# A pacing wait in front of the scatters of a token-routed projection is taken out (one core)

## The reference

```
x = x + 0.5 * ffn(layernorm(x))     # phase 1 of the routed projection, then attention
x = x + encoder_block(layernorm(x)) # 16 heads of 16, relative positions, 2 linear layers
x = x + 0.5 * ffn(layernorm(x))     # phase 2 of the routed projection, then attention

def ffn(x):                         # q, k, v each by a routed two-layer projection
    for f in (q, k, v):
        leaf = walk of a binary tree of depth 4 by the signs of x . node_w[cur] + node_b[cur]
        out_f = relu(x @ w1[leaf] + b1[leaf]) @ w2[leaf] + b2[leaf]   # 256 -> 64 -> 256
    return softmax(q @ k.T / 16) @ v
```

## Time and profile before

| | |
|---|---|
| median of 3 runs | 3535.45 us (3533.83 to 3539.51) |
| the profiled execution | 3535.45 us, span 3533.8 us |
| PE busy | 3043.8 us, 86% of the span |
| DVE busy | 2089.9 us, 59% |
| ACT busy | 1758.2 us, 50% |
| POOL busy | 863.8 us, 24% |
| SP's transfers, share of 16 DMA engines over the span | 33.8% |
| Pool's transfers, same | 7.4% |

### The profile page before, as it was taken

How to read it: one execution, slowest core, us unless ns; L and a number is a source line. 1 busy time by engine, 2 the same in 40 slices (tenths; PEclk the granted TensorE clock), 3 DMA queues, 4 the chain that set the end, 5 groups by cost and what they waited for, 6 DMA issues and landing times. The chain is left out here.

```text
span 3533.8 us, 56088 instructions
## 1 busy us (share of the span) xinstructions
PE 3043.8 (86%) x21058; PEld 1867.1 (53%) x21058; DVE 2089.9 (59%) x3115; ACT 1758.2 (50%) x3413; POOL 863.8 (24%) x1448
## 2 busy tenths in 40 slices
PE   7377579999688999999999999999677377679999
PEld 6256368888343333333333333333346266468888
DVE  3222245544347999999999999995243222245554
ACT  1133233333121888888888888888341133333333
POOL 5531232100013222222222222211025531232100
PEclk9999789999795999999999999999885699789999
DMA  7488421100557444444444455440321488421100
GB/s 259 142 279 249 147 59 52 43 27 20 191 204 88 54 58 56 56 57 56 56 56 56 61 60 61 54 52 9 107 96 50 149 276 255 137 59 53 44 26 22
DMA packets 498902, 338.91 MB, mean 96 GB/s; under 512 B 174333, under 2 KB 473372, under 8 KB 498638
## 3 DMA queue, kind: packets, MB, share of 16 engines
q1 hardware_dynamic: 464718, 251.45, 33.8%
q0 software_dynamic: 33920, 83.93, 7.4%
HBM read 207.93 MB, written 130.97 MB: 96 GB/s over the span
## 5 line engine op out<-in xcount | busy, mean ns | idle before, releaser
L1355 DVE TENSOR_REDUCE mx_ha<-s_ps_ha 128x2 f32<-128x1024 f32 x1024 | 1242.4, 1221 | 106.1 <-PE s_ps_ha L1262 101.8
L1420 ACT ACTIVATE probs_ha<-s_ps_ha 128x512 f32<-128x512 f32 x2048 | 1108.8, 595 | 218.7 <-PE s_ps_ha L1273 84.6
L1262 PE MATMUL s_ps_ha<-ks_ha,qs_ha 48*128 48x512 f32 x2048 | 760.9, 455 | 18.7 <-DMA ks_ha<-parts_d 13.2
L1273 PE MATMUL s_ps_ha<-qs_ha,ks_ha 50*128 50x512 f32 x2048 | 750.7, 446 | 0.9 <-ACT probs_ha L1420 0.2
L1284 PE MATMUL o_ps_ha<-probs_ha,vs_ha 128*32 128x256 f32 (+1 forms) x7936 | 650.1, 400 | 21.4 <-DVE oT_ha L1382 21.4
L1262 PEld LDWEIGHTS s_ps_ha<-ks_ha,qs_ha 48*128 48x128 f32 x2048 | 314.9, 191 | 453.5 <-DVE mx_ha L1355 360.1
L640 PE MATMUL s_ps_a<-kT_a,qT_a 128*128 128x512 f32 x1536 | 398.3, 407 | 2.9 <-issue 2.9
L673 PE MATMUL o_ps_a<-v_a,probsT_a 128*128 128x512 f32 x1024 | 380.4, 411 | 7.2 <-DVE probsT_a L702 6.9
L399 DVE COPY y_p<-y_ps_p 128x256 f32<-128x256 f32 x282 | 117.5, 424 | 447.6 <-PE y_ps_p L496 285.0
L614 POOL DMA_INDIRECT rows_a<-ys_d,slots x192 | 181.7, 946 | 792.7 <-PE turn_ps_a L628 511.6
L1284 PEld LDWEIGHTS o_ps_ha<-probs_ha,vs_ha 128*32 128x32 f32 x7936 | 156.8, 108 | 381.0 <-issue 176.1
(11 more groups left out here) (178 smaller groups left out, 3439.5 us busy)
## 6 DMA issues: line engine op xcount, KB each, us to landing
xs_p<-xs_d SPq DMA_DIRECT2D x66, 512.0 KB
ys_d<-y_p SPq DMA_DIRECT2D x66, 512.0 KB
qs_ha<-parts_d SPq DMA_DIRECT2D x192, 128.0 KB, 6.1
ks_ha<-parts_d SPq DMA_DIRECT2D x192, 128.0 KB, 6.9
wa_p<-in_wa SPq DMA_DIRECT2D x282, 65.5 KB
wb_p<-in_wb SPq DMA_DIRECT2D x282, 65.0 KB
parts_d<-parts_hp POOLq DMA_DIRECT2D x32, 512.0 KB, 3.1
xs_d<-y_p SPq DMA_DIRECT2D x15, 1024.0 KB, 11.1
```

The lines of the kernel that those rows point to most:

```text
L1262: nc.tensor.matmul(s1_ps[:, e % BANKS, :], qs[0:QKROWS, n % SLOTS, c, :], ks[0:QKROWS, n % SLOTS, g * 4:(g + 1) * 4, :].rearrange("p c t - ...
L1273: nc.tensor.matmul(out, ks[LOW:LOW + KR, n % SLOTS, c, :], qs[LOW:LOW + KR, n % SLOTS, g * 4:(g + 1) * 4, :].rearrange("p c t -> p (c t)") ...
L1355: nc.vector.reduce_max(mx[:, at:at + 2], s1_ps[:, e % BANKS:e % BANKS + 2, :], AX_X).then_inc(s1_free, 1)
L1420: nc.scalar.activation(probs[:, (n + c) % (LATE + 1), g * 512:(g + 1) * 512], s2_ps[:, turn % TURNS, :], ACT.Exp).then_inc(s2_free, 1)
```

## The change

The wait of Pool for `turned` in front of the scatters of passes 2 and 3 is removed, in both phases. The waits for the blanking of `xs_d` (first phase only) and for the slots of the pass stay, and so does everything on the other engines.

```diff
@@ -278,8 +278,6 @@
                     pool.wait_ge(filled[f], 16 * -(-SEG // (YB * GROUP)))
                 pool.wait_ge(slot_step, 3 * (k + 1))
                 for t in range(GT):
-                    if k >= 1:
-                        pool.wait_ge(turned, (k - 1) * SEG + t + 1)
                     pool.indirect_dma_start(xs_d[f], bass.IndirectOffsetOnAxis(slots[:, f, t:t + 1], 0),
                                             xn[:, t, :], None).then_inc(scattered[f], 16)
```

## The result

The changed kernel takes 3678.11 us (median of 4 runs, 3675.05 to 3680.67), the kernel before on the same chip 3534.64 (4 runs, 3532.32 to 3539.51). The ratio is 1.0404, 95% interval [1.0385, 1.0422]: 143.5 us slower, where 4.6 was forecast. The profiled execution took 3675.87 us, its span 3674.2.

What follows compares the result with a forecast made beforehand. Projection tiles were taken as paced by DMA landings, with engine demand rising to 1.04 beside dense scatters. Per phase +1.9 us net collision and +0.4 at the start, twice, gave +4.6 on 3535.45: 3540 us, range 3530 to 3553.

Steps and rivals of the forecast that it cites:

- the removed wait is worth 0 by itself: Pool's scatters in the projection: over 20 us of slack each, so starting them earlier gives back no time.
- the term for the collision: Projection tiles beside dense scatters: 8.0 us paid less 6.1 freed, net +1.9 us per phase.
- Pool's 96 scatters in one run ending near 224 us: Pool in each phase: scatters issued unbroken, waits for PE gone, one every 1.265 us.
- The first turn later by less than 1 us: Projection start: three scatters now run before the first `xs` load, costing 0 to 1.0 us, taken as 0.4.
- What is given back: Projection tiles after 224 us run free of scatters: 60.5 tiles by 0.10 us, 6.1 us per phase.
- The term u: Share of time the DMA engines reach beside dense scatters, taken as 0.955: 1.90 us a tile, 8.0 us paid per phase.
- the engine time per tile: DMA engine time one projection tile needs: taken as 21.0 engine-us, between 20.4 and 21.4 from the rows.
- The rule of the Trainium skill: DMA engines go round robin over queues; early scatters would fill gaps, full use, net -2.6 us per phase.
- rival (b): Projection scatters cost the same whenever they come: 3536 us; full engine use without start cost, 3530 us; chance 0.18.
- (c): Faster: a projection tile needs only 20.4 engine-us at full engine use, 2 x -4.7, 3526 us; chance 0.10.
- Rival (a): DMA engines become the projection's bound and stay ragged: +10.6 to +16.6 us, 3546 to 3552 us; chance 0.34.

Runs made afterwards that it cites:

- e1: Changed kernel plus an always-met wait before each of the 64 freed scatters: 3521.68 us on chip 11, 3687.24 us (ratio 1.0416) on chip 4.
- a0: The changed kernel with no line altered, run again on chip 2: 3500.76 us, ratio 0.9987 to the kernel before.

## Why the prediction was wrong

**The failed step** is "So the removed wait is worth 0 by itself. What counts is what the earlier traffic collides with." It took for granted that Pool's issuing, as distinct from its traffic, doesn't touch the other engines. On a chip like the first it does: while Pool issues scatters every 1.265 us without a break, PE's signals reach ACT, DVE and SP 10 us late at first and then 30 to 43, and SP's register instructions are stretched. So the delay of PE's signals, which the sum had at nothing, cost 68.5 and 72.1 us in the two phases, where the term for the collision, +1.9 a phase, has no part: the DMA engines' share was 0.31. Shown: the late signals with prompt answers in the other direction; their place, beside the unbroken run once tiles flow; their size, 75.8 us until the first store, which is all of the loss; that the same program has neither on chip 2. That the old wait protected such a chip is shown by the pair before and after. What in it protects is not: the longer step (1.65 to 1.77 us), the idle time in it, or that Pool waits for PE's own semaphore. e1 excludes only a wait instruction that is met.

**A sign in the trace of before that I passed over.** The kernel before has a stretch with Pool unbroken and PE at work, the start of attention, where gathers follow each other every 1.3 us. ACT's copies of kT come about every 1.3 us too, until they stop coming. DVE, which needs ACT's part, starts at once after ACT (418.50 and 0.38 us, then 418.92), and PE at 419.49 after DVE's end at 419.34. Here DVE receives ACT's signal at once while PE's reach ACT up to 5 us late (turned by 416.63, copied at 422.01), which points to PE's signals and not to receivers in general:

```profile
414.98 0.38 ACT L761 ACTIVATE kT_a<-pT_ps_a 128x256 fp32r<-128x256 f32 x1 [2.00 <-PE pT_ps_a L628]
418.50 0.38 ACT L761 ACTIVATE kT_a<-pT_ps_a 128x256 fp32r<-128x256 f32 x1 [3.14 <-remote]
418.92 0.42 DVE L709 TENSOR_TENSOR kT_a<-pT_ps_a,kT_a 128x256 fp32r<-128x256 f32 x1 [3.10 <-ACT kT_a L761]
422.01 0.38 ACT L761 ACTIVATE kT_a<-pT_ps_a 128x256 fp32r<-128x256 f32 x1 [3.12 <-remote]
```

On chip 2 (a0) the same copies keep their pace to the end:

```profile
413.22 0.38 ACT L759 ACTIVATE kT_a<-pT_ps_a 128x256 fp32r<-128x256 f32 x1 [0.89 <-PE pT_ps_a L626]
414.45 0.38 ACT L759 ACTIVATE kT_a<-pT_ps_a 128x256 fp32r<-128x256 f32 x1 [0.85 <-PE pT_ps_a L626]
415.69 0.38 ACT L759 ACTIVATE kT_a<-pT_ps_a 128x256 fp32r<-128x256 f32 x1 [0.86 <-PE pT_ps_a L626]
```

From the first gather to the first softmax row the first chip takes 40.2 us (396.55 to ACT at 436.77), chip 2, in the changed kernel, 35.4 (392.13 to 427.50); in the second phase they take 40.6 and 35.6. And in the trace of before SP's MOVE already took up to 700 ns, though 29 is its median:

```profile
L208 SPq MOVE wb_p<-in_wb x282: 1/29/700, 104.5 to 3035.7; - x141
```

The long ones lie beside paced scatters (603 ns in 160 to 200 us, 629 in 237 to 287); without scatters (290 to 390 us) all 58 take 29 ns. So what may be the same effect already showed beside the paced scatters.

**The steps that held.** Pool's 96 scatters in one run ending near 224 us: 222.84. The first turn later by less than 1 us: 148.8 against 148.2 us. "What is given back", 6.1 us a phase: on the first chip, where no scatter meets a running loop any more, the stretch from first store to first gather shrank from 234.0 to 226.7 us, 7.3. It contains a few tiles made ahead during the stall (the first four after it take 6.5 us), so the agreement with 6.1 is rough.

**The term u.** Where the loss doesn't come, the prediction's own sum can be checked. It chose 0.955 by the rows of before, since "1.00 is not seen over 40 us". That reading was wrong for the trace as a whole: before the tile loop, while x is loaded and `xs_d` blanked, the kernel before has

```profile
40.00:80.00 40.00, 35.59 (x186) 31.26 (x186) 16.50 (x72) 4.94 (x7) 22.82 (x29) 1.00 1.04 344
```

In the dense stretch of phase 1, e1 (chip 11) and a0 (chip 2) have 1.00, and a0's tile takes 1.756 us where the working gave 1.78 for u = 1.00 and 1.90 for 0.955. In phase 2 a0 has 0.94 and 1.836 us a tile, where the working gives about 1.94. So u was too low for one phase and close for the other, and the engine time per tile was too high in both: (16 x 1.00 - 4.2) x 1.756 = 20.7 and (16 x 0.94 - 4.2) x 1.836 = 19.9, where 21.0 was taken. The rule of the Trainium skill (*DMA: Bandwidth & Descriptors*, "Queues, rings and completion order"), that each DMA engine takes packets from its queues in turn, was read as full use; phase 1 agrees with that reading (1.00), phase 2 doesn't (0.94).

The rival (b) at u = 1.00 had 2 x -2.6 = -5.2 us; chip 2 measured -6.1 by the medians, its interval reaching from -9.5 to +0.4. That the two are close is partly luck, as u was 1.00 in one phase only; the interval holds (c) at -9.4 too, and leaves out the forecast of +4.6. No trace of the kernel before was taken on that chip, so the parts of these 6 us are only argued. Rival (a), saturation, had the right sign and the wrong cause: the engines were saturated only where nothing was lost.

**Open:** what distinguishes the two kinds of chip (or of placement on one), where the signals are held, whether a pause, a compute operation or the plain form of transfer between the scatters prevents it, and what share of the 21 to 33 us between the kernels before on the two kinds comes from the same cause; the attention start accounts for some 5 us a phase. What in Pool's issuing holds the signals up wasn't isolated.

## What to carry to other kernels

A wait that looks free to remove may be what keeps an engine's transfers from disturbing the others: before removing it, look in the trace for any other stretch where Pool issues indirect transfers back to back beside working engines, and look there for idle times that end "remote" long after the producer ended. Time such a change on more than one chip, with the unchanged kernel beside it on each; an experiment that shows no loss proves nothing about a cure unless the loss was shown on that same chip. The wait is worth keeping here: on chip 2 it costs 6 us (interval 9.5 to -0.4), and it saves 140 on the first chip and on chip 4; leaving only the third set free (3499.7 beside 3513.4, one run each) was not tried on a chip that shows the loss.

## What the runs showed of the hardware that was not expected

- One program, two kinds of chip: 3678.1 and 3678.9 us against 3500.8; the kernel before 3534.6 and 3538.7 against 3506 to 3513 on four others, two of which ran a kernel known to lose.
- On the slower kind, beside indirect transfers issued by Pool every 1.265 us, PE's signals arrive in order, 5 to 12 us apart and up to 43 us late (tile 5, turned by 170.25, is copied at 213.07), those of ACT promptly; DVE's were prompt beside the gathers (419.34 to 419.49). A tile takes 22.4 us in place of 1.75. The backlog outlasts Pool's last transfer by 12 us.
- Beside dense scatters the 16 DMA engines reach 1.00 of their time over 40 us in phase 1 on chips 2 and 11 (337 and 334 GB/s), where the spaced scatters had shown 0.93; in phase 2 on chip 2 the same scatters show 0.94.
